# Cross-attention kernel: the third text chunk of a batch moved into the next batch, queries projected at the end of a batch

## What is computed

```
q = x @ w_q;  k, v = text @ w_k, text @ w_v;  k_ip, v_ip = ip @ w_k_ip, ip @ w_v_ip
out_text = softmax(q k^T / 4) v
out_ip   = softmax(q k_ip^T / 4 + mask(box)) v_ip
out = (out_text + out_ip) @ w_out + b_out + x
```

## Time and profile before

| what | us |
|---|---|
| median of three runs | 210.18 (210.06 to 210.33) |
| the profiled execution | 210.0 |
| its span, first to last instruction | 208.2 |

### The profile page before, as it was taken

How to read it: one execution, slowest core, us unless ns; L and a number is a source line. 1 busy time by engine, 2 the same in 40 slices (tenths; PEclk the granted TensorE clock), 3 DMA queues, 4 the chain that set the end, 5 groups by cost and what they waited for, 6 DMA issues and landing times.

```text
span 208.2 us, 4662 instructions
## 1 busy us (share of the span) xinstructions
PE 182.1 (87%) x1608; PEld 148.4 (71%) x1608; DVE 147.8 (71%) x355; ACT 129.3 (62%) x298; POOL 103.9 (50%) x107
## 2 busy tenths in 40 slices
PE   0895999999967989999989999999999978998971
PEld 0775999999965648777666958676795946766741
DVE  1668562366827687877968797978779799778482
ACT  4529363342337967955794797389378749849640
POOL 7004029601360758655683786577376546638200
PEclk9999599999999999999999999999999999999999
DMA  5999798899982575784785756578754772220301
GB/s 146 274 404 359 268 341 192 191 241 295 226 201 77 136 176 131 239 190 112 203 241 145 227 164 191 127 214 274 164 159 134 232 160 84 63 74 0 100 30 63
DMA packets 35814, 37.72 MB, mean 181 GB/s; under 512 B 11216, under 2 KB 34000, under 8 KB 35792
## 3 DMA queue, kind: packets, MB, share of 16 engines
q1 hardware_dynamic: 35792, 37.44, 63.8%
HBM read 25.63 MB, written 11.47 MB: 178 GB/s over the span
## 4 chain that ended last, share of the span: by engine, by line
PE 32%; SPq 18%; DVE 17%; DMA 15%; ACT 8%; issue 6%; POOL 3%; DVEq 0%; ACTq 0%; POOLq 0%
PE bank L420 20%; SPq L298 8%; DVE negmax L1049 6%; DMA x_raw<-xT 4%; DMA raw<-wk_ip 4%; SPq L316 4%; DMA vr<-vip_dram 3%; PE bank L570 3%; ACT raw L826 3%; PE bank L584 3%; PE bank L492 3%; PE bank L525 2%; DVE pip L973 2%; DMA q_dram<-q_l 2%; DVE q_l L973 2%
## 5 line engine op out<-in xcount | busy, mean ns | idle before, releaser
L1049 DVE TENSOR_REDUCE negmax<-bank 128x4 f32<-128x448 f32 x80 | 49.9, 623 | 22.5 <-PE bank L492 22.0
L826 ACT ACTIVATE raw<-bank 112x512 f32<-112x512 f32 x80 | 46.4, 599 | 2.9 <-PE bank L525 1.6
L1199 POOL TENSOR_TENSOR x_l<-x_raw,x_h 128x768 fp32r<-128x768 f32 x8 | 15.3, 1916 | 20.5 <-ACT x_h L763 20.5
L570 PE MATMUL bank<-raw,v 112*32 112x256 f32 x320 | 22.2, 385 | 1.2 <-DVE late L1095 0.4
L1250 POOL TENSOR_TENSOR late<-late 128x256 f32<-128x256 f32 x20 | 14.7, 733 | 17.0 <-DVE late L1095 17.0
L584 PE MATMUL bank<-raw,con 112*32 112x256 f32 x320 | 22.1, 382 | 0.0
L420 PE MATMUL bank<-ctx_hl,key_w 128*128 128x448 f32 x72 | 16.9, 398 | 5.8 <-DVE ctx_hl L973 5.8
L420 PE MATMUL bank<-wo_h,ctx_hl 128*128 128x320 f32 x80 | 19.8, 317 | 2.4 <-DVE ctx_hl L973 2.4
L1199 POOL TENSOR_TENSOR ctx_hl<-late,ctx_hl 128x256 fp32r<-128x256 f32 x20 | 14.7, 737 | 13.7 <-ACT ctx_hl L853 10.2
L492 PE MATMUL bank<-key_w 96*128 96x240 f32 x80 | 17.1, 305 | 4.6 <-DVE ips L1052 1.9
L868 ACT ACTIVATE log_z<-bank 128x256 f32<-128x256 f32 x24 | 9.2, 384 | 17.7 <-PE bank L584 17.5
(11 more groups left out here) (103 smaller groups left out, 463.6 us busy)
## 6 DMA issues: line engine op xcount, KB each, us to landing
x_raw<-xT SPq DMA_DIRECT2D x8, 384.0 KB, 4.4
q_dram<-q_h SPq DMA_DIRECT2D x8, 384.0 KB, 3.8
q_dram<-q_l SPq DMA_DIRECT2D x8, 384.0 KB, 3.5
late<-x SPq DMA_DIRECT2D x8, 320.0 KB, 3.4
out<-late SPq DMA_DIRECT2D x8, 320.0 KB, 2.5
qs<-q_dram SPq DMA_DIRECT2D x12, 192.0 KB, 3.4
k_dram<-late SPq DMA_DIRECT2D x4, 480.0 KB, 3.9
key_w<-q_dram SPq DMA_DIRECT2D x9, 192.0 KB, 3.5
```

The lines of the kernel that those rows point to most:

```text
L570: mm = pe.matmul(oz_bank[(k + c) % 2][32 * j:32 * j + 32, 0:S], v[k][:, 2 * p + ab, :], probs[:, p, S * ab:S * ab + S], start=n < 4, stop= ...
L826: nc.scalar.activation(probs[:, p, :], b_banks(b)[p % len(b_banks(b))][0:TEXT, :], ACT.Exp, scale=SCALE).then_inc(p_done, 1)
L1049: nc.vector.tensor_reduce(negmax[:, t, :, 2 * g:2 * g + 2].rearrange("p a q -> p q a"), s[:, :, 0:TEXT].rearrange("p (q a) n -> p q a n", ...
L1199: sub = lambda o, a, b: nc.gpsimd.tensor_tensor(o, a, b, ALU.subtract)
```

## The change

Three things change place; no arithmetic does.

- **Third text chunk.** For batches with b + 2 <= 7 (`deferred`) PE does chunk 2 of batch b in step b + 1, behind its second pair of scores (`late_chunk`). ACT makes its seed behind `probabilities(b, 1)`, DVE normalises it behind the third read (the second one in step 6) and ahead of `low_ip(b, k, 0)`, POOL adds it last in its step, behind `residual`.
- **Queries.** project_q(b + 3) stands at the end of step b, behind text chunk 1, instead of project_q(b + 2) at the start. It waits for the output of batch b - 1 to be out of the banks. `high_q` and `low_q` move along.
- **Image transposes.** In steps 1 to 5 only part 0 stays behind pair 1; part 1 (four transposes) comes behind text_out 0, since its bank is used by the late chunk. ACT's `high_ip` of part 1 moves behind pair 4 and `high_out(b - 1, 2)`, DVE's `low_ip` of part 1 behind two more reads.

```
+        def deferred(b):
+
+            return b >= 0 and exists(b + 2)
...
# PE, step
-                if exists(b - 1) and exists(b + 2):
-                    pe.wait_ge(sl_done, c)
-                    pe.wait_ge(oi_done, 2 * b)
-
-                    pe.wait_ge(ot_done, XC * b - 2)
-                    project_q(b + 2)
...
+                def late_chunk():
+                    text_out(b - 1, 1 - k, 2)
+                    text_sums(b - 1, 1 - k, 2)
...
                     if exists(b + 2):
                         more_a(1)
                         both(1)
+                        late_chunk()
+                        pe.wait_ge(ot_done, XC * b - 1)
                         transpose_ip(b, k, 0)
-                        transpose_ip(b, k, 1)
                         both(2)
                         both(3)
                     elif exists(c):
 
                         score_b(b, k, 1)
                         more_a(2)
+                        late_chunk()
+                        pe.wait_ge(y_done, QT * (b - 1))
                         transpose_ip(b, k, 0)
                         transpose_ip(b, k, 1)
...
                 both(4)
                 text_out(b, k, 0)
+                if exists(b - 1) and exists(b + 2):
+                    pe.wait_ge(ot_done, XC * b)
+                    transpose_ip(b, k, 1)
                 both(5)
...
-                for chunk in (1, 2):
-                    text_out(b, k, chunk)
-                    text_sums(b, k, chunk)
+                text_out(b, k, 1)
+                text_sums(b, k, 1)
+                if exists(b + 3):
+                    pe.wait_ge(y_done, QT * b)
+                    pe.wait_ge(oi_done, 2 * (b + 1))
+                    pe.wait_ge(ql_done, 2 * (b + 3))
+                    project_q(b + 3)
+                if not deferred(b):
+                    text_out(b, k, 2)
+                    text_sums(b, k, 2)
...
# ACT, step
-                if exists(b + 2):
+                if not exists(b - 1):
                     high_q(b + 2, 0)
-                    if exists(b - 1):
+                    high_q(b + 2, 1)
+                else:
+                    probabilities(b, 0)
+                    if exists(b + 2):
                         high_out(b - 1, 1)
-                    high_q(b + 2, 1)
-                if exists(b - 1):
-                    probabilities(b, 0)
                     probabilities(b, 1)
+                    if deferred(b - 1):
+                        seed(b - 1, 1 - k, 2)
...
                 probabilities(b, 4)
+                if exists(b - 1):
+                    high_out(b - 1, 2)
+                if exists(b - 1) and exists(b + 2):
+                    high_ip(b, k, 1)
                 values(c, 1 - k)
...
                 high_out(b, 0)
-                seed(b, k, 2)
+                if exists(b + 3):
+                    high_q(b + 3, 0)
+                    high_q(b + 3, 1)
+                if not deferred(b):
+                    seed(b, k, 2)
...
# DVE, step
+                if deferred(b - 1):
+                    some_a(3 if exists(b + 2) else 2)
+                    normalise(b - 1, 1 - k, 2)
+                    low_ip(b, k, 0)
+                    some_a(2)
+                    low_ip(b, k, 1)
+                else:
...
                     normalise(b, k, 1)
-                    normalise(b, k, 2)
+                    if exists(b + 3):
+                        low_q(b + 3, 0)
+                        low_q(b + 3, 1)
+                    if not deferred(b):
+                        normalise(b, k, 2)
...
# POOL, step
                     output(b, 1)
-                    if exists(b + 2):
-                        output(b, 2)
                 residual(b)
+                if deferred(b):
+                    output(b, 2)
```

More of the change, by code:

```diff
@@ L637, in step @@
                     score_b(b, k, 0)
-                    if exists(b + 2):
-                        pe.wait_ge(ot_done, XC * b)
-                    else:
-                        pe.wait_ge(y_done, QT * (b - 1))
+                    if exists(c):
                         pe.wait_ge(sl_done, c)
@@ L659, in step @@
                     else:
+                        pe.wait_ge(y_done, QT * (b - 1))
+                        pe.wait_ge(sl_done, c)
                         for p in (1, 2, 3):
@@ L885, in step @@
                 high_ip(b, k, 0)
-                high_ip(b, k, 1)
+                if not (exists(b - 1) and exists(b + 2)):
+                    high_ip(b, k, 1)
                 if not exists(b - 1):
@@ L893, in step @@
                 probabilities(b, 3)
-                if exists(b - 1):
-                    high_out(b - 1, 2)
                 if exists(b + 3):
@@ L1133, in step @@
                     add_image(b - 1, 2)
-                some_a(2)
-                low_ip(b, k, 0)
-                some_a(1)
-                low_ip(b, k, 1)
-                some_a(1)
-                if exists(b + 2):
-                    low_q(b + 2, 0)
-                    low_q(b + 2, 1)
-                some_a(1)
+                if deferred(b - 1):
[5 more added lines that the diff above has]
+                else:
+                    some_a(2)
+                    low_ip(b, k, 0)
+                    some_a(1)
+                    low_ip(b, k, 1)
+                    some_a(1)
+                    if not exists(b - 1):
+                        low_q(b + 2, 0)
+                        low_q(b + 2, 1)
                 if not exists(c):
@@ L1145, in step @@
                     last_chunk_out(b - 1)
-                some_a(5)
+                some_a(10)
                 if exists(c):
```

## The result

The changed kernel takes 218.13 us (median of four runs, 215.53 to 224.14), beside 210.12 for the kernel before: a ratio of 1.0345, with a 95% interval of 1.0252 to 1.0438. Medians in this document are of all runs, while a ratio compares only the runs within 1.5% of their kernel's fastest with those of the kernel before from the same rounds, so it can differ from the quotient of two medians. The forecast was 210.6 with a range of 207.8 to 213.2. The sign was the likelier one, the size is outside the range by 4.9 us. The profiled execution took 218.25 us, with a span of 216.4 against 208.2.

What follows compares the result with a forecast made beforehand. PE had the largest share, with SP's queue and transfers a third; PE, ACT and DVE shared the score stage. Step 0 -1.40, steps 1-4 -0.12, x +0.40, step 5 -0.05, step 6 +1.63: +0.46, giving 210.6 us (207.8 to 213.2).

Steps and rivals of the forecast that it cites:

- The walk: The prediction's instruction-by-instruction timing of a changed step: 18.59 us, with a 0.8 us PE stall ahead of text chunk 0.
- Score stage: Step's zero to the first output projection, steps 1 to 4: predicted 1.46 us longer, on 9.71; bounds 0 and +0.4 more.
- P0: First output projection of a step, ending the score stage: predicted at 11.17 us after zero.
- zero: Start of each step as the prediction cuts the span: the first b-score of each batch.
- End stage: From P0 to the next zero: predicted 7.42 us instead of 8.57, new waits free; step 0 gives back 1.40.
- The x load: Key loads to x load taken as 10.8 us, as in step 0; 0.1 us lateness per step, +0.4 in all.
- my rival on the x load: x lands late in steps 2 to 4, about 0.45 us each: +1.3 more, 212.0 us; chance 0.17.
- one of my signs of being wrong: ACT's wait for x_raw: over 0.8 us would show the forecast wrong.
- The rival on the shift load: The shift load binds all steps, next zero at 19.16 over 18.59: 213.7 us; chance 0.12.
- Step 5: Bound by the second shift load, landing at 16.44 after zero: 16.48 us against 16.53, -0.05.
- Step 6: Batch 5's chunk 2 lands here with nothing given back; fifth a-score at 5.45 instead of 3.82: +1.63 us.
- The faster rival: PE's work decides, no stall ahead of chunk 0: steps of 18.08, 207.0 us; chance 0.30 including half of it, 208.9.

Runs made afterwards that it cites:

- repaired kernel: Changed kernel with VectorE's low image half ahead of the late normalisation and batch 5's third chunk kept in its own batch: 210.24 us, again 209.32 us.
- e8: Repaired kernel with ScalarE making the values ahead of the high half of image part 1: 211.86 us, ratio 1.0141.
- e2: Changed kernel with six extra matmuls, result unused, filling PE's pause ahead of text chunk 0 in steps 1 to 5: 215.43 us, ratio 1.0259.
- e5: Changed kernel with batch 5's third text chunk left in its own batch: 218.91 us.
- e11: Repaired kernel with four extra matmuls, result unused, ahead of the fifth a-score in steps 1 to 5: 210.82 us, ratio 1.0097.
- e1: Changed kernel with VectorE taking the low image half ahead of the late normalisation: 213.53 us, ratio 1.0112.
- e6: Changed kernel with both repairs, low image half first and batch 5's third chunk in its own batch: 210.24 us, ratio 0.9949.
- e13: The same kernel as e6 measured once more, twelve runs: 209.32 us, ratio 1.0026.
- e4: Kernel before with only the third text chunk moved, queries still projected at the start of a step: 224.42 us, ratio 1.0653.
- e7: Kernel before with only two unused VectorE additions of 230 columns ahead of the low image half in steps 1 to 5: 234.1 us, ratio 1.111.
- e14: Kernel before with the third read first, then three unused VectorE maxima ahead of the low image half in steps 1 to 5: 221.42 us, ratio 1.0599.
- e3: Kernel before with only the query projection moved; third chunk and transposes stay: 222.65 us, runs from 214.49 to 234.25, inconclusive as a time.
- e12: Kernel before with one unused VectorE reduction over 448 columns ahead of the low image half in steps 1 to 5: 211.6 us, ratio 1.016.

## Why the prediction was wrong, step by step

- **The clock was no term.** "PE is busy for 17.5 us of an undisturbed step, at the full granted clock": the column was read, and then taken as a constant of the kernel. All my prices for a pause were its own length; no rival had the engine running slower afterwards. This is the step that failed: some 6.6 of the 7.7 us by which the span missed its forecast. The walk had even found the stall, "0.8 us on PE, all of it DVE's order". The Trainium skill, "TensorE: Matmul & The Clock Gate", section "What's actually happening", says that the throttled state is the default and that activity releases it; the traces fit this as far as they go (0.54 in the window that begins where PE returns from the pauses), and I hadn't asked of a change that opens a pause in every step what it does to that.
- **Score stage, the mechanism right, the size 0.5 short.** The pause ahead of chunk 0 is 0.79 to 0.83 us in steps 1 to 5 (predicted 0.8), but P0 is 11.67 after zero in step 1, for 11.17. Chunk 0 starts 5.37 after zero and not 4.97: the normalisation begins 0.14 later (the third a-score, behind the late chunk and two transposes, starts 2.19 after zero, not 2.05), takes 1.37 and not 1.26, and PE starts 0.67 after the start of the low image half, for which I had 0.51. From pair 5 to P0 it is 4.60 for 4.44. I had named +0.4 as the upper bound and took zero. Over four steps this is +1.6 us against the walk with its 0.40 for x. In the repaired kernel e8 gained nothing by taking ACT's wait for the transposes out of the way of the values.
- **End stage right.** 7.46 us in step 1, predicted 7.42; the new waits at the projection cost nothing. Step 0 gives back 1.37, predicted 1.40.
- **The x load: wrong in its mechanism, and hidden.** The walk took step 0 as the model, where six key loads take 2.68 us, and gave as the reason that the store ahead of them comes early. In steps 1 and 2 at the full clock the store came 2.1 us ahead, and they took 3.42 and 3.97, where I had named under 3.2 as a sign of being right; they take 2.68 only from step 3 on, where the low clock puts them 1.5 us later:

```profile
82.81 0.49 SPq L312 DMA_DIRECT2D q_dram<-q_l  x1
84.86 3.42 SPq L302 DMA_DIRECT2D key_w<-k_dram  x6
...
104.00 3.97 SPq L302 DMA_DIRECT2D ks<-k_dram  x6
...
124.52 2.68 SPq L302 DMA_DIRECT2D key_w<-k_dram  x6
```

  From the key loads to the x load it is 11.83 us in step 1 and 11.73 in step 2, not 10.8, and over the 11.6 from which my rival on the x load decides. ACT waits 0.19 us for x in step 2 and 1.07 in step 3 (1.28 in step 2 before), one of my signs of being wrong:

```profile
120.84 0.62 ACT L776 CAST x_h<-x_raw 128x512 fp32r<-128x512 f32 x1 [1.07 <-DMA x_raw<-xT]
```

  It still costs nothing: step 3 takes 20.44 us with this wait and step 4 20.45 without one. So the rival was right in its condition and wrong in its price of 0.45 a step, and that my 0.40 for x did little harm is luck. The rival on the shift load falls: no first b-score of steps 1 to 5 waits for it in the changed kernel.

- **Step 5: the landing right, P0 not.** The second shift load takes 2.62 us and lands 5.30 after P0 (169.49; predicted 16.44 - 11.17 = 5.27), and the first b-score of step 6 starts 5.35 after it (predicted 5.31):

```profile
172.17 2.62 DMA qs<-shift
```

  So the step is longer by what its P0 is later: 17.12 in e2 at the full clock, for 16.48.
- **Step 6.** The fifth a-score starts 5.72 after zero (180.56 - 174.84), predicted 5.45: +1.90 and not +1.63. The pause of 1.84 us there, with those of step 5 before it, is followed by the longest low stretch, which begins 2.1 us after PE's return: the clock of the step is 0.83. e5 takes the chunk out of it and step 6 takes 17.07 us at the full clock; but e8 and e11, also without the chunk, show that the clock can fall there all the same.
- **The faster rival** ("if the normalisation got ahead of chunk 0 without a stall") gives 18.08 for a step; e1, which removes the stall, has 18.51. With batch 5 kept as well (e6) it is 18.34. The rival's 207.0 us is 0.985 of the 210.18 it started from; e6 came out at 0.9949 and the same kernel in e13 at 1.0026, and neither interval reaches 0.985.
- **The noise was larger than I took it.** "A measurement of this kernel tells 0.2%" went by three runs within 0.13%. The later runs of the same kernel spread over 3.8% (206.19 to 213.94 us). The change of 3.5% is clear of no change by its interval, but a forecast of +0.46 us would not have been told from none by four runs.

Open: why steps 1 and 2 keep the clock and steps 3 to 5 lose it with the same pauses, and why e4 keeps it in steps 1 to 5. In the changed kernel and in e5 the low stretches of steps 3 to 5 begin 5.6 to 5.9 us after zero each time, so the moment at which a pause falls may matter beside its length; no run moves the same pauses in time, and this rival is untested. Open too: step 6 with the late chunk at the full clock, which no run had; and whether the late chunk's light matmuls add to what the pauses do, which no run separates from them at an equal pause. The sizes of the clock's terms in steps 5 and 6 are worked out as rests, not measured alone.

## What to carry to other kernels

When a walk finds a new pause on TensorE in every step of a loop, price it twice: its own length, and a low stretch that may follow (here 1.4 us for one of 3.4 us, in some steps), and write the second down as a rival with a chance. On the engine that feeds TensorE, put what TensorE waits for ahead of the rest: here one exchange of two calls on DVE was worth 4.6 us of the 8 lost, in part by the clock. And read the clock column beside the busy share, since a PE at the lower clock is busy too (18.91 of 20.44 us in step 3, 17.53 of 19.13 in step 1).

## What the runs showed of the hardware

**The clock after short pauses.** In the profiled executions pauses of up to 1.2 us a step didn't lower it in steps 1 to 5, pauses of 1.5 to 1.9 us lowered it in some of them, and one of 2.2 us in one piece in all five (e7); e4 kept it with 1.7 to 2.6 us in pieces. A low stretch of 3.4 us cost 1.36 us of time (20.44 for 19.09), one of 6.8 us in e14 2.9 (22.39 for 19.49), one of 10.2 us in e3 4.1 (23.83 for 19.77). It isn't reproducible from step to step: the same instructions with the same pauses went either way within one execution. The Trainium skill, "TensorE: Matmul & The Clock Gate", section "HAM oscillation — how this bites in real kernels", describes the clock going down in the wait for a DMA in each turn of a loop, with waits of 3 to 5 us; here pauses of 0.3 to 1.2 us, none by itself near that, did it (changed kernel, e3, e14).

**A DVE operation with two SBUF operands against POOL.** The same addition of 230 columns, twice in a row in e7, and POOL beside it:

```profile
104.40 1.54 DVE L1137 TENSOR_TENSOR wq_raw<-con 128x230 f32<-128x230 f32 x1
105.86 0.39 DVE L1137 TENSOR_TENSOR wv_raw<-con 128x230 f32<-128x230 f32 x1
...
104.11 1.57 POOL L1244 TENSOR_TENSOR xb<-late,bias 128x640 f32<-128x640 f32 x1
```

The first took 1.54 us and ended 0.26 us after POOL's addition (105.68), the second 0.39; in all five steps it is 1.49 to 1.54 for the first and 0.38 to 0.39 for the second. That is why e7's pause was 2.22 us instead of 1.2. The Trainium skill, "SBUF — State Buffer", section "SBUF: two separate sides", says that DVE and GpSimd share a pair of ports as an exclusive lock, which an operation of DVE with two SBUF operands takes, and that the later one is blocked until the other has ended. The trace agrees: 1.54 for 0.39 us. e12 and e14 use a reduction with one operand for that reason: in e12 it took 0.61 us in each of the five steps, each begun 0.3 us into the same addition of POOL.
